# The value products of the fourth key block moved to stand directly behind those of the second, one step earlier

## The reference, cut to what matters

```python
q = x @ wq_lat @ wq_heads
k = x @ wk_lat @ wk_heads
v = x @ wv_lat @ wv_heads
q = q.reshape(Bx, Tx, N_HEAD, HEAD_DIM).transpose(0, 2, 1, 3)
...
att = jnp.einsum('bhqd,bhkd->bhqk', q, k) * SCALE
causal = jnp.tril(jnp.ones((Tx, Tx), dtype=bool))
att = jnp.where(causal[None, None], att, -jnp.inf)
att = jax.nn.softmax(att, axis=-1)
y = jnp.einsum('bhqk,bhkd->bhqd', att, v)
```

## Time and profile before

| | us |
|---|---|
| median of 3 runs | 1187.3 |
| lowest and highest of them | 1186.52, 1191.24 |
| the profiled execution | 1182.42 |
| its span, first to last instruction | 1180.7 |
| PE busy | 1019.0 (86%) |
| DVE busy | 830.3 (70%) |
| ACT busy | 742.6 (63%) |
| POOL busy | 632.6 (54%) |

### The profile page before, as it was taken

How to read it: one execution, slowest core, us unless ns; L and a number is a source line. 1 busy time by engine, 2 the same in 40 slices (tenths; PEclk the granted TensorE clock), 3 DMA queues, 4 the chain that set the end, 5 groups by cost and what they waited for, 6 DMA issues and landing times. The chain is left out here.

```text
span 1180.7 us, 31510 instructions
## 1 busy us (share of the span) xinstructions
PE 1019.0 (86%) x8446; PEld 608.8 (52%) x8446; DVE 830.3 (70%) x2411; ACT 742.6 (63%) x1311; POOL 632.6 (54%) x1195
## 2 busy tenths in 40 slices
PE   4488888988888898987788998866999999999875
PEld 3453333333333333333345665535888888888732
DVE  5677887778777877777779998433666666666637
ACT  4577777777777767775655666414666666666616
POOL 4236666666666666664423777771444444444344
PEclk9899999999999999998996999878999999999988
DMA  8313333333332333333243111112222222221166
GB/s 217 94 47 93 99 96 103 95 100 87 97 108 86 99 95 99 100 99 111 71 150 115 54 54 57 54 60 68 61 64 64 64 58 63 62 65 54 43 224 210
DMA packets 135606, 107.47 MB, mean 91 GB/s; under 512 B 32203, under 2 KB 127874, under 8 KB 135538
## 3 DMA queue, kind: packets, MB, share of 16 engines
q1 hardware_dynamic: 124722, 87.45, 26.3%
q0 software_dynamic: 8544, 17.78, 4.2%
q10 hardware_dynamic: 2272, 1.45, 0.4%
HBM read 55.96 MB, written 50.69 MB: 90 GB/s over the span
## 5 line engine op out<-in xcount | busy, mean ns | idle before, releaser
L1542 DVE TENSOR_REDUCE maxima<-ps 128x8 f32<-128x1024 f32 x320 | 381.2, 1220 | 119.4 <-PE ps L1164 107.3
L916 ACT ACTIVATE pT_area<-ps 128x1024 f32<-128x1024 f32 x320 | 327.1, 1024 | 138.0 <-PE ps L1196 136.8
L704 POOL TENSOR_SCALAR_AFFINE_SELECT pT_area<-pT_area 128x256 f32<-128x256 f32 (+1 forms) x448 | 190.3, 439 | 103.7 <-ACT pT_area L916 103.2
L806 POOL DMA_INDIRECT ys_dram<-quad_area,place_cur x139 | 133.0, 957 | 192.6 <-issue 135.7
L1237 PE MATMUL ps<-pT_area,quad_area 128*32 128x512 f32 (+3 forms) x2048 | 190.7, 446 | 0.0
L796 POOL DMA_INDIRECT xs_dram<-quad_area,idx_cur x128 | 123.1, 962 | 74.9 <-issue 73.6
L1196 PE MATMUL ps<-quad_area 64*128 64x512 bf16 (+3 forms) x1024 | 125.5, 302 | 39.4 <-DVE maxima L1542 37.9
L1404 PE MATMUL ps<-quad_area 128*128 128x256 f32 (+1 forms) x456 | 130.0, 367 | 6.3 <-issue 4.5
L1405 PE MATMUL ps<-quad_area 128*128 128x256 f32 (+1 forms) x456 | 128.5, 364 | 0.0
L1164 PE MATMUL ps<-quad_area 61*128 61x128 bf16 (+2 forms) x1792 | 126.2, 242 | 0.0
L1024 ACT ACTIVATE xnT<-ps,be_cur 128x256 f32<-128x256 f32 (+1 forms) x228 | 94.4, 447 | 47.6 <-PE ps L1405 47.3
(11 more groups left out here) (237 smaller groups left out, 1523.1 us busy)
## 6 DMA issues: line engine op xcount, KB each, us to landing
qk_dram<-split_area SPq DMA_DIRECT2D x192, 128.0 KB, 2.3
quad_area<-qk_dram SPq DMA_DIRECT2D x256, 96.0 KB, 2.3
row_area<-xs_dram SPq DMA_DIRECT2D x63, 132.0 KB
pT_area<-ys_dram SPq DMA_DIRECT2D x16, 512.0 KB, 5.0
pT_area<-in_L_ffn_We SPq DMA_DIRECT2D x12, 384.0 KB, 7.0
out_dram<-pT_area SPq DMA_DIRECT2D x7, 512.0 KB, 2.9
xs_dram<-row_area SPq DMA_DIRECT2D x5, 528.0 KB, 4.2
split_area<-in_L_ffn_We SPq DMA_DIRECT2D x12, 192.0 KB, 3.6
```

Of the source, the lines that this page charges most:

```text
L704: return pool.affine_select(out=blocks, in_=blocks, compare_op=ALU.is_ge, fill=0.0, base=0, pattern=[[0, count], [1, P]], channel_multipli ...
L806: pool.indirect_dma_start(ys_dram, at, ys[:, ns % 2, h, :], None).then_inc(s_yst[ns % 2], 16)
L916: act.activation(pT[:, gs % 2, n, :], ps[:, bank:bank + 2, :].rearrange("p a b -> p (a b)"), ACT.Exp).then_inc(s_exp, 1)
L1542: dve.tensor_reduce(to, ps[:, bank:bank + 2, :].rearrange("p a (j k) -> p a j k", k=P), AX, ALU.max).then_inc(s_mxf, 1)
```

## The change

The kb 3 products are no longer done one step later behind exp 0, but in the same step as the other three, directly behind kb 1, which reads the same units 1 and 3 of `pT`. The order within a quad becomes 0, 1, 3, 2. `LAST_READ` is worked out from that order, and the matmul that closes a PSUM sum is the one of kb 2 now. The kb 3 products also carry a wait on POOL's masks, for the same count as kb 1 directly ahead of them.

```diff
-PRODUCTS = {("exp", 0): (2, 3), ("exp", 2): (1, 0), ("exp", 3): (1, 1), ("exp", 4): (1, 2)}
-LAST_READ = (0, 3, 0, 3, 2)
+PRODUCTS = {("exp", 2): (0,), ("exp", 3): (1, 3), ("exp", 4): (2,)}
+PRODUCT_ORDER = (0, 1, 3, 2)
+LAST_READ = tuple(PRODUCT_ORDER.index(kb) for kb in (0, 3, 0, 3, 2))
...
-                if kb < 3:
-                    pe.wait_ge(s_masked, UNITS * g + 3 + kb)
+                pe.wait_ge(s_masked, UNITS * g + (3, 4, 5, 4)[kb])
...
-                    if (kind, n) in PRODUCTS:
-                        late, kb = PRODUCTS[kind, n]
-                        if 0 <= gs - late < QUADS:
-                            products(gs - late, g - late, kb)
+                        for kb in PRODUCTS[kind, n]:
+                            if 0 <= gs - 1 < QUADS:
+                                products(gs - 1, g - 1, kb)
```

More of the change, by code:

```diff
@@ L1237, in products @@
                     last = pe.matmul(ps[32 * i:32 * i + 32, bank, kb * P:T], v_cur[:, slot, kb, i, :],
-                                     pT[:, buf, n, 512 * rg + at:512 * rg + at + w], start=(kb == 0 and gs % 2 == 0), stop=(kb == 3 and gs % 2 == 1))
+                                     pT[:, buf, n, 512 * rg + at:512 * rg + at + w], start=(kb == 0 and gs % 2 == 0), stop=(kb == PRODUCT_ORDER[-1] and gs % 2 == 1))
                 last.then_inc(s_pv, 1)
```

## The result

| | before | changed |
|---|---|---|
| median, 20 runs each, us | 1185.66 | 1190.89 |
| lowest and highest | 1181.08, 1191.24 | 1184.88, 1195.93 |
| span of the profiled execution | 1180.7 | 1189.2 |
| one turn of the loop (four steps), in the profiles | 33.10 | 33.26 |

The ratio is 1.0041 with a 95% interval from 1.0027 to 1.0056: the changed kernel is 3.2 to 6.6 us slower, real but under half a percent. Forecast were +3.4 us and no change that can be told at 0.5%.

The account below looks back on a forecast made before the run. DVE was taken to lead each step's first half, PE the second, at least in even steps. Third steps 2.9, first steps 0.7 and tail -0.2 gave +3.4 us on 1187.3: 1190.7 us, range 1185.5 to 1196.5.

Parts of the forecast that it names:

- the rhythm: Loop of four-step turns: 2.9 us from third steps and 0.7 from first steps; turn from 33.10 to 33.36 us.
- the tail: Last steps and closing block of products, where PE leads: -0.45, +0.43 and -0.21 give -0.2 us.
- Part 1, the relief behind exp 0: Taking kb 3 from behind exp 0 relieves PE of some 0.45 us a step but saves 0 time.
- The price of a group behind a group: Kb 3 directly behind kb 1: a 128-column group costs 0.21 us there, at most 0.36.
- Rival A: A group behind a group costs what it costs alone, 0.36 us: +8.5 us, 1195.8; chance 0.15.
- The third step: Third step of a turn: max 4, join and next max 0 all move 0.21 us, 14 times, 2.9 us.
- The first step: First step of a turn: slack of 0.16 ahead of exp 4 leaves 0.05 us, 13 times, 0.7 us.
- The fourth: Fourth step of a turn: PE's wait for DVE at exp 0 takes up the added group; 0.
- The second: Second step of a turn: PE's wait ahead of max 0 takes up the added group; 0.
- the -0.45: In the tail: saving from kb 3 no longer standing behind exp 0 of the last full step, 0.45 us.
- B: PE's saving counts: 0.24 us net in each of 64 steps, 15.4 us faster, 1171.9; chance 0.06.
- C: The delay is swallowed wholly by waits of DVE or for a load; 1187.1, the tail alone; chance 0.17.

Follow-up runs that it names:

- the kernels with and without that rest in the first step: With: the changed kernel, mean 1190.99 us. Without: the changed kernel with kb 3 back behind exp 0 in one step of four, 1188.32 us.
- the kernel with the extra group: The kernel before with a second kb 3 group added behind kb 1, the old one staying behind exp 0; 1190.43 us, ratio 1.0050.
- The change on the faster base: The studied change made on the kernel before with kb 0 behind max 3 and kb 2 behind the projection; 1182.85 us, that base 1170.54.

## Why the prediction was right, and where it wasn't

**The sign and the size** were right: +3.4 us forecast, 3.2 to 6.6 measured. But the sum was right partly by luck, through errors of opposite sign: the rhythm was put 1.4 us too high (3.6 forecast, 2.2 measured), the tail 0.4 too low, and some 2 us of the clock were not in the sum at all. Without the falls of the clock the change would have cost about 2.4 us.

**Part 1, the relief behind exp 0, worth 0.** The time of the rhythm bears it out: without kb 3 the turn is 33.08. That it is worth nothing is still not what happened: it costs. With PE resting there the clock falls now and then in the first step, 1.5 us each time (10.0 against 8.47). This is the step of the working that failed. It read "what is late next" from the waits and took the granted clock of 1.00 for given. Two falls, as in two of the three profiles, are 3 us, none, as in the third, is 0; the timed runs say 2.1, with an error of some 0.8, between the kernels with and without that rest in the first step. That all of it is these falls is not shown, and the kernel with the extra group, whose clock held, was slower than its turn accounts for, by a microsecond or two that stay open.

**The price of a group behind a group, 0.21** from the block at the end: measured 0.23 and 0.22. Rival A, 0.36, has fallen.

**The third step, 0.21, 14 times.** The mechanism held, the size didn't: 7.14 against 7.00 us, 0.14. The join starts at 326.84 and max 0 at 327.09, 0.25 later; I called that "without a pause". In the changed kernel it is 332.17 to 332.34, 0.17. The missing 0.08 was a wait for PE's fill of max 0, too short to be listed: its last matmuls end at 326.65 + 0.39 = 327.04. 2.0 us, not 2.9.

**The first step, 0.05**: 8.47 against 8.42, exactly; the slack ahead of exp 4 was read rightly. **The fourth**: 8.55 in both. **The second**: 9.10 against 9.13, 0.03 less than the zero I took. Together 0.16 a turn where 0.26 was forecast.

**The tail, -0.2.** The sign was wrong. From the first exp 2 of the last step with a maxima transpose to the last turn of sums it is 611.23 - 596.10 = 15.13 us, and was 605.77 - 590.81 = 14.96. PE in the changed kernel, at exp 0 and exp 1 of the last full step, and the block of four groups:

```profile
601.05 0.39 PE L1197 MATMUL ps<-quad_area 64*128 64x512 bf16 x2
601.66 0.39 PE L1197 MATMUL ps<-quad_area 64*128 64x384 bf16 x4 [0.23 <-ACT pT_area L917]
...
608.11 2.36 PE L1237 MATMUL ps<-pT_area,quad_area 128*32 128x512 f32 x32
```

The block shrank by 0.22 as forecast (2.36 against 2.58 in the earlier trace rows), but behind exp 0 only 0.07 of 0.45 was saved (0.61 from exp 0 to exp 1, and 0.68 before): exp 1 waits for ACT. So the mis-sized term is the -0.45. The relief was worth almost as little here as elsewhere.

**The sum as measured**: 14 x 0.16 = 2.2 us of rhythm, 0.2 of tail, 2.1 of clock, 4.5 in all, against 4.9 from the ratio (3.2 to 6.6) and 5.2 from all runs, each against the kernel before beside it. The clock's term comes from such runs itself, so that the sum comes out is no second proof of it.

**The rivals.** B had its case in the fourth step, whose exp 2 showed no wait; it fell with the kernel without kb 3. The rule of the Trainium skill, page TensorEngine Tiling (Array Packing), Key Properties, on the drain at a change of tiling mode agrees in its direction with what PE saved, 1.2 us of busy time in a turn; nothing was waiting for it. C, that all is swallowed, would have held but for the 0.14 of the third step and the 0.05 of the first.

## What to carry to other kernels

Read who leads in each stretch of a rhythm, and price a move by the wait it meets there: the same group of 0.22 us, once in each of four steps, cost 0.15 to 0.87 us a turn by its place and base, and its removal from a stretch led by another engine gave nothing. The first place to look is work that stands ahead of a fill for which the next engine idles; moving three product groups behind such fills took 22 us off. And filler in front of a wait is not free to remove: on TensorE it may be what holds the clock.

## What the runs showed of the hardware

Groups of products in the same column tiles follow each other at 0.21 to 0.23 us for 128 columns, while one alone between groups in other tiles takes 0.36 to its successor, and its predecessor takes 0.09 more.

The granted clock fell in the loop eleven times, each time at the same place of the rhythm, in kernels whose PE stood still 0.29 to 0.58, 0.75 to 0.84 and 0.35 us in short succession ahead of it; no single one of these waits was as long as a microsecond. In the kernel before they are 0.58, 0.38 and 0.35 with kb 3 between the first two, and nothing falls. These waits stand ahead of exp 2 in nearly every first step of the changed kernel, and most of those steps show no fall. Which of the turns it takes varies from run to run: two in one profile of the changed kernel, none in the next. The Trainium skill, page TensorE: Matmul & The Clock Gate, Part 1, says that the chip grants the full clock by how busy the engine has been of late, and that the phase of this watch against the kernel varies. The trace agrees with the first in its direction: all eleven falls came in kernels in which PE had less to do in that place (the row from 172.00 against the one from 169.05). The second would explain that only some turns are hit; no trace here shows the phase. The change on the faster base bears on what the work has to be: there kb 3 is gone from behind exp 0 as well, and PE waits 0.75 to 0.87 and 0.35 us, but not ahead of exp 0, and nothing falls. So it need not be a product in that very place. That PE's work as such holds the clock is still inferred from the kernels; a filler that is no product was not tried.
